# Scores and values of two steps made at once, and the banks laid out anew, in a fused Mamba and transformer kernel

## The reference

```python
q, k, v = jnp.split(shift_tokens(x) @ Wqkv, 3, -1)      # 16 heads of 64
q = l2norm(q) * qs; k = l2norm(k) * ksc
q = q * cos * scale + rotate_half(q) * sin * scale
k = k * cos / scale + rotate_half(k) * sin / scale
# windows of 32 tokens; each sees itself and the window before it
sim = jnp.einsum('bhwie,bhwje->bhwij', bq, bk2) * 8.0
sim = jnp.where(mask, -big, sim)
attn = jax.nn.softmax(sim, -1)
out = jnp.einsum('bhwij,bhwje->bhwie', attn, bv2)
x = out @ Wo + x
x = (gate/up/down of layernorm(shift_tokens(x))) + x
```

## Time and profile before

| | us |
|---|---|
| median of 3 runs | 2067.97 (2062.97 to 2070.41) |
| the profiled execution | 2066.36 |
| its span, first to last instruction | 2064.6 |
| TensorE busy in it | 1989.6 (96%) |
| VectorE busy | 1518.1 (74%) |
| ScalarE busy | 1383.4 (67%) |
| GpSimd busy | 1225.6 (59%) |

### The profile page before, as it was taken

One profiled execution on the slowest core, in us unless ns is written; L12 is line 12 of the kernel. 1 busy time (PEld: TensorE's weight loads), 2 busy tenths in 40 slices (PEclk: granted clock), 3 DMA queues, 4 the chain that ended last, 5 costly groups with the idle time before them and its releaser, 6 DMA issues.

```text
span 2064.6 us, 82312 instructions
## 1 busy us (share of the span) xinstructions
PE 1989.6 (96%) x33044; PEld 1399.8 (68%) x33044; DVE 1518.1 (74%) x2875; ACT 1383.4 (67%) x4164; POOL 1225.6 (59%) x1374
## 2 busy tenths in 40 slices
PE   7789798999999999999999999999999999999998
PEld 3333233887686786876876877868768778687684
DVE  1499897886796776867867967769678678686783
ACT  4533233886786777767867867768678677776783
POOL 1376774775584565765746855648557567565570
PEclk9888989999999999999999999999999999999999
DMA  1321110311131111121211311112211111111110
GB/s 62 134 72 70 63 61 0 105 44 38 39 90 42 40 43 39 45 77 36 53 37 37 96 38 41 44 32 50 76 47 43 40 39 49 38 43 33 24 40 22
DMA packets 148091, 104.30 MB, mean 51 GB/s; under 512 B 15778, under 2 KB 140256, under 8 KB 146176
## 3 DMA queue, kind: packets, MB, share of 16 engines
q1 hardware_dynamic: 147712, 99.07, 17.3%
HBM read 48.31 MB, written 1.18 MB: 24 GB/s over the span
## 4 chain that ended last, share of the span: by engine, by line
PE 82%; issue 0%; POOL 0%; ACT 0%; DVE 0%; POOLq 0%; ACTq 0%
PE ps L1033 20%; PE ps L1040 9%; PE ps L1019 8%; PE ps L1058 8%; PE ps L1000 8%; PE ps L981 7%; PE ps L1054 4%; PE ps L958 4%; PE ps L1098 3%; PE ps L1092 3%; PE ps L1103 3%; PE ps L975 2%; PE ps L1078 1%; PE ps L1087 1%; PE ps L1133 0%
## 5 line engine op out<-in xcount | busy, mean ns | idle before, releaser
L1510 POOL TENSOR_TENSOR QK<-QK,RN 128x512 f32<-128x512 f32 x384 | 400.8, 1044 | 374.2 <-ACT RN L1223 359.1
L1233 ACT ACTIVATE PR<-ps,MN 128x64 f32<-128x64 f32 x1536 | 357.3, 316 | 154.6 <-DVE MN L1361 139.8
L1033 PE MATMUL ps<-W,XS 128*128 128x256 f32 x1536 | 435.3, 406 | 4.9 <-PEq L64 4.1
L1505 POOL TENSOR_TENSOR QK<-PC,PS 128x256 f32<-128x256 f32 x384 | 280.7, 731 | 246.4 <-PE ps L1019 243.7
L1259 ACT COPY QKT<-ps 128x512 f32<-128x512 f32 x384 | 225.0, 586 | 248.6 <-PE ps L1019 248.6
L1385 DVE TENSOR_REDUCE SS<-SQ 128x8 f32<-128x512 f32 x384 | 262.3, 683 | 58.0 <-ACT SQ L1266 55.2
L1033 PEld LDWEIGHTS ps<-W,XS 128*128 128x128 f32 x1536 | 261.0, 189 | 61.5 <-issue 4.9
L1506 POOL TENSOR_TENSOR QK<-PC,PS 128x256 f32<-128x256 f32 x384 | 281.3, 733 | 0.0
L1361 DVE TENSOR_REDUCE MN<-ps 128x4 f32<-128x256 f32 x384 | 163.0, 424 | 149.8 <-PE ps L981 148.5
L1404 DVE TENSOR_TENSOR PC<-ps,TC 128x512 f32<-128x512 f32 x384 | 261.4, 681 | 0.1
L1406 DVE TENSOR_TENSOR PS<-ps,TS 128x512 f32<-128x512 f32 x384 | 260.7, 679 | 0.0
(11 more groups left out here) (142 smaller groups left out, 3226.7 us busy)
## 6 DMA issues: line engine op xcount, KB each, us to landing
V<-V SPq DMA_DIRECT2D x384, 97.5 KB, 2.2
scr<-B_rows SPq DMA_DIRECT2D x32, 512.0 KB, 3.5
V<-V SPq DMA_DIRECT2D x288, 32.5 KB, 2.4
W<-in_Wqkv SPq DMA_DIRECT2D x40, 192.0 KB, 2.8
TC<-in_tcos SPq DMA_DIRECT2D x6, 1024.0 KB, 5.9
TS<-in_tsin SPq DMA_DIRECT2D x6, 1024.0 KB, 8.5
WO<-in_Wo SPq DMA_DIRECT2D x6, 512.0 KB, 4.1
W<-in_W SPq DMA_DIRECT2D x6, 341.0 KB
```

Source lines behind the costliest of these rows:

```text
L1033: mm = nc.tensor.matmul(ps[:, par, k * 2 * P:(k + 1) * 2 * P], cols[k], W[:, i, 0:2, :].rearrange("p t m -> p (t m)"), start=True, stop=True)
L1233: e = nc.scalar.activation(PR[:, m % 2, h, slot * DH:(slot + 1) * DH], ps[:, 3 + h, slot * DH:(slot + 1) * DH], ACT.Exp, scale=-1.0, bias= ...
L1505: nc.gpsimd.tensor_tensor(QK[:, par, :, 0:hd], PC[:, par, :, 0:hd], PS[:, par, :, hd:DH], ALU.add)
L1510: nc.gpsimd.tensor_tensor(QK[:, par, :, :], QK[:, par, :, :], bcast_last(RN[:, m // 2 % 2, 8 * par:8 * par + 8], DH), ALU.mult).then_inc(q ...
```

## The change

Every even step now makes scores and values of two steps, the odd step none.

- `scores`: at even `n` for the steps `n-6` and `n-5`. The mask is one product of 256 columns per bank, from a table of three blocks (`MASKB`), then 32 small products. The scores take columns 0 to 255 of banks 3 and 4.
- `least` reads both at once (128x512), at even `n`, into `MN`. `exponents` still runs each step, one step later than before.
- `values`: at even `n` for `n-8` and `n-7`, in columns 0 to 259 of banks 5 and 6. `normalise` takes one reciprocal for both and two products.
- v's projection moves to bank 4 (256 to 511), into a function of its own (`project_v`). The transposed output moves to columns 256 to 511 of bank 3, the transposed probabilities to the last 128 columns of banks 5 and 6.
- On TensorE both transposes of q and k (`qk_transposed`) stand in the even step, the second behind the projection of q and k.
- On VectorE an even step's order is `least`, `clamp_pair`, `tables`, `normalise`, `norms`. Before, `normalise` stood ahead of `clamp_pair` and `tables`.
- On ScalarE `norm_pair` moves to the even step, ahead of the exponents, and the order of the copies differs between even and odd steps.
- The waits follow the banks: see the diff. The work placed by `U_...` moves one step later, and the pipeline drains in 9 steps instead of 8.

```diff
-U_WO, U_MEAN, U_DEV, U_VAR, U_INV, U_Z, U_FFN, U_TAB = (6, 8), (7, 9), (8, 10), (10, 12), (11, 13), (12, 14), 16, 17
+U_WO, U_MEAN, U_DEV, U_VAR, U_INV, U_Z, U_FFN, U_TAB = (7, 9), (8, 10), (9, 11), (11, 13), (12, 14), (13, 15), 17, 17
...
             def out_transposed(n):
-                m = n - 8
+                m = n - 9
...
                 pe.wait_ge(on, m + 1)
                 for k in range(2):
+                    if steady(n) and n % 2 == 1 and k == 1:
+                        pe.wait_ge(v_cp, n)
...
             def scores(n):
-                m = n - 5
-                if not 0 <= m < NSTEPS:
+                if n % 2 or not 0 <= n - 6 < NSTEPS:
                     return
...
                 for h in range(2):
+                    if h == 0:
+                        pe.wait_ge(v_cp, min(n, NSTEPS))
...
-                    nc.tensor.matmul(ps[:, 3 + h, 0:P], identb[:], MASKB[:, int(s == 0), h, :], start=True, stop=True)
+                    nc.tensor.matmul(ps[:, 3 + h, 0:2 * P].rearrange("p (f c) -> p f c", f=2), identb[:],
+                                     MASKB[:, f:f + 2, h, :], start=True, stop=True)
...
+                for m in (n - 6, n - 5):
...
             def values(n):
...
+                pe.wait_ge(pT, n - 6)
+                for m in (n - 8, n - 7):
...
             def project(n):
...
                 for k in range(2):
+                    if k == 1 and n % 2 == 0:
+                        wait(pe, mn, n - 4)
...
+            def project_v(n):
...
-                wait(pe, on, n - 6)
+                wait(pe, pr, n - 5)
                 for k in range(2):
-                    mm = nc.tensor.matmul(ps[:, 5, (2 + k) * P:(3 + k) * P], cols[k], W[:, i, 2, :], start=True, stop=True)
+                    if steady(n) and n % 2 == 1 and k == 1:
+                        pe.wait_ge(pT, n - 6)
+                    mm = nc.tensor.matmul(ps[:, 4, (2 + k) * P:(3 + k) * P], cols[k], W[:, i, 2, :], start=True, stop=True)
...
             def p_transposed(n):
...
-                    wait(pe, on, m)
                     pe.wait_ge(pr, m + 1)
+                wait(pe, on, min(n - 6 - n % 2, NSTEPS))
...
             def exponents(n):
-                m = n - 5
+                m = n - 6
...
                 wait(act, pT_ps, m - 1)
+                if m % 2:
+                    wait(act, oT_ps, min(n - 8, NSTEPS))
...
             for n in range(DRAIN):
...
-                norm_pair(n)
-                copy_qk(n)
-                exponents(n)
+                if n % 2 == 0:
+                    copy_qk(n)
+                    norm_pair(n)
+                    exponents(n)
+                    copy_out(n)
+                    squares(n)
+                    copy_v(n)
+                else:
+                    exponents(n)
+                    copy_p(n - 1)
+                    copy_qk(n)
...
                 least(n)
-                normalise(n)
                 clamp_pair(n)
                 tables(n)
+                normalise(n)
                 norms(n)
```

More of the change, by code:

```diff
@@ L689, in _ @@
             pool.wait_ge(s_id, 1)
-            nc.gpsimd.tensor_copy(MASKB[:].rearrange("p f h c -> p (f h c)"), MASK).then_inc(s_half, 1)
-            nc.gpsimd.tensor_copy(identb[:], ident[:])
+            for f, first in enumerate((1, 0, 0)):
+                nc.gpsimd.tensor_copy(MASKB[:, f, :, :].rearrange("p h c -> p (h c)"), MASK[:, first * 2 * P:(first + 1) * 2 * P])
+            nc.gpsimd.tensor_copy(identb[:], ident[:]).then_inc(s_half, 1)
             pool.wait_ge(ld_qks, 16)
@@ L976, in scores @@
                 if steady(n):
[L977 to L984, removed]
@@ L985, in scores @@
-                mm.then_inc(s_ps, 1)
+                    pe.wait_ge(v_sh[(n - 7) % 4], 32 * ((n - 7) // 4 + 1))
+                for m in (n - 6, n - 5):
+                    s = place(m)[3]
+                    for slot in range(2):
+                        for h, quad in spread_tiles:
+                            c0 = PAD + s * STEP + window(slot, quad) * WIN
+                            o0 = (m % 2) * P + slot * DH
+                            mm = nc.tensor.matmul(ps[32 * quad:32 * quad + 32, 3 + h, o0:o0 + DH],
+                                                  QKT[DH * h:DH * h + DH, 0, c0:c0 + WIN],
+                                                  QKT[DH * h:DH * h + DH, 1, c0 - WIN:c0 + WIN],
+                                                  start=False, stop=True, skip_group_check=True)
+                    mm.then_inc(s_ps, 1)
@@ L987, in values @@
             def values(n):
-                m = n - 7
-                if not 0 <= m < NSTEPS:
+                if n % 2 or not 0 <= n - 8 < NSTEPS:
                     return
                 if not steady(n):
-                    pe.wait_ge(pT, m + 1)
-                    pe.wait_ge(v_sh[m % 4], 32 * (m // 4 + 1))
-                    wait(pe, on, m)
[L995 to L1000, removed]
-                                              PT[r, m % 2, h, 32 * quad:32 * quad + 32],
-                                              V[r, 2 * (m % 8) + j // 4, 2 * (1 - j % 2) + h, :], start=True, stop=True)
@@ L1003, in values @@
-                mm.then_inc(o_ps, 1)
+                    for m in (n - 8, n - 7):
+                        pe.wait_ge(v_sh[m % 4], 32 * (m // 4 + 1))
+                    wait(pe, on, n - 8)
+                pe.wait_ge(pT, n - 6)
+                for m in (n - 8, n - 7):
+                    for h in range(2):
+                        for slot, quad in spread_tiles:
+                            j = window(slot, quad)
+                            r = slice(64 * slot, 64 * slot + 64)
+                            o0 = (2 * (m % 2) + h) * (DH + 1)
+                            mm = nc.tensor.matmul(ps[32 * quad:32 * quad + 32, 5 + slot, o0:o0 + DH + 1],
+                                                  PT[r, m % 2, h, 32 * quad:32 * quad + 32],
+                                                  V[r, 2 * (m % 8) + j // 4, 2 * (1 - j % 2) + h, :], start=True, stop=True)
+                    mm.then_inc(o_ps, 1)
@@ L1008, in qk_transposed @@
                     return
-                if not steady(n):
+                if not steady(n) or n % 2:
                     wait(pe, qkT, m)
```

115 lines of the change are left out of this document (62 added, 53 removed).

## The result

The changed kernel takes 2336.65 us (2335.16 to 2337.09, 3 runs) against 2067.97 us. The ratio is 1.130, with a 95% interval of 1.127 to 1.134. The sign and the ring of waits were right. The size was not: 165 us were forecast, 269 came, and the time lies above the range.

What follows compares the result with a forecast made beforehand. TensorE alone bounds the kernel before; the change closes a ring of waits, +0.92 us a pair: 191 pairs give 176, phases -9, drain +2, start -4, so +165 on 2066.4: 2231 us, range 2150 to 2275.

Steps and rivals of the forecast that it cites:

- the ring of waits: Waits within one pair of steps close a ring across TensorE, VectorE and ScalarE: 7.48 us a pair against 6.56; chance 0.78.
- two routes: To the second output transpose: over VectorE's normalised values V + 3.55, over even exponents and v's copy V + 3.68; later counts.
- the signs that I named: Plain pair 7.3-7.7 us; minimum 0.3, reciprocal 2.2 behind values; ScalarE idle 0.3 and over 1; TensorE's chain share below 82%.
- V: Start of the even step's values on TensorE, from which the ring's times are counted.
- step 6: Odd step's exponents wait for the second output transpose (shared bank 3), which ends 0.27 us later: V + 3.95.
- step 8: On TensorE the mask takes 0.11 + 0.20 us and both steps' scores 0.51, up to the next values.
- the ring is shorter: Rival: the ring's operations alone are 7.14 us, and hand-overs cost nothing: 2166 us; chance 0.11.
- The rule on packs: A pack of small matmuls lasts one matmul plus about 4 ns per further tile: total 130 us more, not 165.
- TensorE's saving: Fewer turns between full products and small tiles save TensorE 0.44 us a pair: 6.12 if it stayed the bound.
- the "faster" rival: Rival: waits are met and TensorE's turns decide, a pair takes 6.12 us: 1982 us; chance 0.05.
- The clock: Rival: TensorE's clock falls with its gaps; a tenth of pairs at 1.2 GHz add 89 us: 2320; chance 0.04.
- Beside the plain pairs: Extra work per phase (output projections, norms, feed-forward, inverses) changes the ring's cost by -0.8 us, -9 us over eleven phases.

Runs made afterwards that it cites:

- A cut of 0.54 us a step on ScalarE: Kernel before the change with one exponent activation of 128x256 with one bias a step in place of four: 2062.7 us, ratio 0.998.
- The orders alone and together: Changed kernel with ScalarE's norm activations at the even step's end, VectorE normalising ahead of the rotary products, or both: 2334.1, 2328.3 and 2279.0 us.
- the single exponent: Changed kernel with one exponent activation of 128x256 with one bias a step in place of four: 2221.8 us, ratio 1.075.
- the bank: Changed kernel with the transposed output in bank 7 where free, so the odd step's exponents don't wait for it: 2274.7 us, ratio 1.101.
- the bank with the orders: Changed kernel with transposed output in bank 7 where free, normalising ahead of rotary products, norm activations right behind even exponents: 2222.7 us, ratio 1.075.
- the old order: Changed kernel with VectorE normalising ahead of the clamp and the rotary products, as before the change: 2510.6 us, ratio 1.215.
- the kernel with most of the ring taken away: Changed kernel with bank 7 for transposed output where free, both reorderings on VectorE and ScalarE, and one exponent activation a step: 2126.9 us, ratio 1.028.
- the filler: Changed kernel with an unread 128x512 product between the older and younger step's scores, in steps that leave bank 7 free: 2442.8 us.
- the run with more scores: Changed kernel with the younger step's 32 score products made twice: 2495.2 us.

## Why the prediction was right in sign and wrong in size

**What bounds the kernel before: right.** A cut of 0.54 us a step on ScalarE gives 3 us there, and TensorE has the chain.

**The ring, its members and its two routes: right.** The exponents of the even step, v's projection, its copy, the output's transposes, the odd exponents and the last copy of v follow each other as laid out, each within 0.1 us up to the second output transpose. The orders alone and together, the single exponent and the bank gave 3, 8, 58, 115 and 62 us for 20, 0 to 10, 57, 120 and 68; the bank with the orders 114 for 99; the old order cost 174 for 210 to 230. Of the signs that I named, VectorE's two (0.35 and 2.23 us behind V), both of ScalarE's idle times (1.46 and 0.50 us) and TensorE's share of the chain came. The length of a plain pair didn't: 7.95, where I gave 7.3 to 7.7.

**The size of the ring: wrong, by 0.47 us in 7.48.** Two terms carry it. In step 6 I let the exponents start 0.27 us behind the second transpose, and they start 0.45 behind its weights: 0.18. The transpose ends 0.33 us behind its weights and not 0.27, and ScalarE starts 0.12 behind that modelled end. I had put this hand-over at nothing, though the prediction itself says that a waiting engine wakes 0.04 to 0.12 us late in every row of before. In step 8 both steps' scores take 0.67 us and not 0.51: 0.16. I took the second 32 at the pace of the first, and the earlier trace rows spoke against it: the values, which are the second 32 there, spread over 0.35 us where the scores take 0.24. I booked that as the price of values and not of their place. The rest are 0.07 at the copy of v, 0.05 ahead of the mask and 0.02 at the turn. On 191 pairs 0.47 us are 90 us, and 9 more are the waits of the values for their own issue. 2231 + 99 = 2330, against 2335 for the profiled execution.

**The range was drawn on the wrong side.** I let it reach down to a ring without hand-overs (2150) and up by a mere 0.25 us a pair. But this ring sums some fifteen durations and seven hand-overs, and all five misses in it went the same way. The rival "the ring is shorter" had no partner "the ring is longer", and that was the one that came.

**The rule on packs: the trace was right against it, and went further.** The span model that I cited from TensorE: Matmul & The Clock Gate of the Trainium skill (Measured speedup vs the span model) has about 4 ns for each further tile, an estimated 0.2 us less than I took. Measured were 0.16 us more.

**TensorE's saving: 0.44 us summed, an estimated 0.15 to 0.25 found.** It lay off the path here, but the "faster" rival rested on it. What was wrong is the pace again: in the kernel with most of the ring taken away the scores take 0.61 to 0.67 us to the values for my 0.51, and the values 0.90 to the next product for my 0.85. (The sum has 0.03 for the scores where the text beside it says 0.02.)

**The clock: no effect,** as forecast. The granted clock is 1.00 over 1880 us of the steps, though single products wait there for up to 0.9 us for the exponents and up to 2.1 us for nothing that the profile shows.

**Beside the plain pairs: right in sum.** By the masks' starts, medians over the phases, the pairs with projections, norms and feed-forward lengthen by 1.18, 0.92, 0.92, 1.79, 1.69, 1.19 and 1.19 us, where a plain one lengthens by 1.39. That is 0.85 us a phase less than seven plain pairs, and I had 0.8. Over eleven phases it is about the 9 us that the waits for issue add back.

## What to carry to other kernels

Batching two steps on the engine that sets the pace takes away the distance between a stage and its consumer: count for each wait how much work lies between what signals and what waits, in the same loop turn, and sum the ring that closes before counting what the batch saves. Give every hand-over of such a ring its price; here the five misses all made it longer, so the range should have reached further above the sum. Price a small product by its place in the stream, not by its name. Where a shared PSUM bank ties two stages, a free bank in part of the steps is a cheap test of it. And an edit that moves one engine's work can put it beside another's: look at what runs at the same time, as with the clamp here.

## What the runs showed of the hardware

Small products started faster when something long ran ahead of them. The first 32 scores (64 rows, 32 columns, 64 moving) start within 0.24 us, some 7.5 ns apart; the next 32 take 0.34 to 0.41 without such a break, whether they are scores (changed kernel) or values (kernel before); and behind a product of 0.86 us they are fast again (the filler). TensorE: Matmul & The Clock Gate of the Trainium skill (Architectural detail: the array is 16x 32x32, not 1x 128x128) states a queue of 64 entries for TensorE; 32 products with their weight loads are 64 instructions, and the trace agrees with it in that the pace falls just behind the first 32. That the queue is the cause isn't shown: the third 32 of a stream take 0.27 us.

A stream of 160 small products in a row (the run with more scores) made TensorE stand still for up to 2.4 us, 63 times, with nothing to wait for in the profile. With 128 it happened 8 times, and with 64 hardly ever (0.8 us in 4 times, ahead of weight loads). That these are instructions which come too late is what it looks like; no run here took it apart.

VectorE's clamp, an operation of 128x16 from SBUF to SBUF, takes 0.16 us alone. Beside a GpSimd operation it took up to 0.9 us. In the kernel before, the changed kernel and the two with the norm's activations at the end of the even step 229 clamps took over 0.25 us, and each ended 0.03 to 0.04 us behind the end of the GpSimd operation that ran.
